# A graph kernel whose attention passes pick three rows in four groups on TensorE, with the weighed values in PSUM and the decays in SBUF

## The reference

```python
h = max(layernorm(x), 0); x = x + sage2(h)             # two passes: sums
h = max(layernorm(x), 0); x = x + transformer2(h)      # two attention passes
h = max(layernorm(x), 0); x = x + graph_transformer(h) # one attention pass, with an edge bias
h = max(layernorm(x), 0); x = x + gin2(h)              # two passes: maxima

# one attention layer
alpha = sum(q[dst] * k[src], -1) * scale     # (edges, 8)
m     = segment_max(alpha, dst)
a     = exp(alpha - m[dst]);  a = a / segment_sum(a, dst)[dst]
out   = segment_sum(v[src] * a[:, :, None], dst)
```

## Time and profile before

| | us |
|---|---|
| median of 3 runs | 8551.9 |
| lowest and highest | 8509.88, 8577.97 |
| the profiled execution | 8522.77 |
| its span | 8520.5 |
| PE busy with matmuls | 5177.5 (29027 matmuls) |
| DVE busy | 5170.0 |
| POOL busy | 4941.0 |
| ACT busy | 2588.6 |

### The profile page before, as it was taken

One profiled execution on the slowest core, in us unless ns is written; L12 is line 12 of the kernel. 1 busy time (PEld: TensorE's weight loads), 2 busy tenths in 40 slices (PEclk: granted clock), 3 DMA queues, 4 the chain that ended last, 5 costly groups with the idle time before them and its releaser, 6 DMA issues.

```text
span 8520.5 us, 85738 instructions
## 1 busy us (share of the span) xinstructions
PE 5177.5 (61%) x29027; PEld 3050.1 (36%) x29027; DVE 5170.0 (61%) x9372; ACT 2588.6 (30%) x6303; POOL 4941.0 (58%) x5102
## 2 busy tenths in 40 slices
PE   4767658887455555355455344454536888768887
PEld 2333334444333333133333233333323444434443
DVE  6666545555677777677777777777773333333333
ACT  3333311111344544354444444444440000000000
POOL 6666665555455665455655555555536555565555
PEclk8777878888777766677766666666657888778887
DMA  4444434444344444344444344444424455445544
GB/s 128 143 140 142 138 118 162 162 163 154 113 145 147 153 148 151 121 146 144 150 145 142 123 142 135 146 134 145 134 72 144 161 162 163 133 142 163 163 162 133
DMA packets 464201, 1216.31 MB, mean 143 GB/s; under 512 B 109489, under 2 KB 142271, under 8 KB 463752
## 3 DMA queue, kind: packets, MB, share of 16 engines
q1 hardware_dynamic: 263180, 721.75, 24.3%
q0 software_dynamic: 200576, 489.04, 20.0%
HBM read 736.73 MB, written 473.62 MB: 142 GB/s over the span
## 4 chain that ended last, share of the span: by engine, by line
PE 43%; issue 31%; DVE 12%; another core or an unknown queue 6%; ACT 4%; DMA 3%; POOL 0%; SPq 0%; DVEq 0%; POOLq 0%; ACTq 0%
PE banks_ps L1630 14%; PE banks_ps L1614 14%; PE cout_ps L1614 5%; PE pair_ps L1614 5%; PE cin_ps L1614 4%; DVE outs L758 2%; ACT outs L1356 1%; DVE hot_both L812 1%; DVE bias L776 1%; DVE work L776 1%; DMA hot_small<-kept_hots 1%; DVE work L896 1%; DMA hot_both<-kept_hots 1%; DVE arena L786 1%
## 5 line engine op out<-in xcount | busy, mean ns | idle before, releaser
L1967 POOL DMA_INDIRECT arena<-table,near_idx x4732 | 4593.8, 971 | 2965.9 <-issue 1412.4
L1614 PE MATMUL banks_ps<-arena,work 128*128 128x384 bf16 x6750 | 1328.1, 348 | 388.1 <-issue 299.4
L1614 PEld LDWEIGHTS banks_ps<-arena,work 128*128 128x128 fp8e4 (+1 forms) x6750 | 681.9, 102 | 988.5 <-issue 624.6
L850 DVE COPY_PREDICATED pair_ps<-near_late,pair_ps 128x896 f32<-128x896 uint8 x336 | 368.5, 1097 | 853.9 <-ACT pair_ps L1375 752.5
L1630 PE MATMUL banks_ps<-arena,hot_small 128*128 128x256 bf16 x2025 | 619.9, 306 | 361.2 <-issue 360.4
L1630 PE MATMUL banks_ps<-work,hot_small 128*128 128x256 bf16 x2025 | 620.5, 306 | 357.8 <-issue 357.0
L896 DVE TENSOR_TENSOR_SCAN work<-banks_ps,work 128x1024 f32<-128x1024 f32 x336 | 769.7, 2291 | 11.5
L786 DVE TENSOR_REDUCE arena<-banks_ps 128x128 f32<-128x384 f32 x324 | 179.6, 554 | 974.1 <-remote 808.2
L1630 PE MATMUL banks_ps<-arena,hot_both 128*128 128x256 bf16 x2025 | 619.8, 306 | 233.4 <-issue 233.0
L1630 PE MATMUL banks_ps<-work,hot_both 128*128 128x256 bf16 x2025 | 618.1, 305 | 229.9 <-issue 229.8
L1299 ACT COPY near_idx<-src_i 128x7 int32<-128x7 int32 x784 | 150.7, 194 | 1953.1 <-DVE outs L758 1713.4
(11 more groups left out here) (267 smaller groups left out, 8634.7 us busy)
## 6 DMA issues: line engine op xcount, KB each, us to landing
rows_plain<-outs SPq DMA_DIRECT2D x448, 448.0 KB
work<-kept_hots SPq DMA_DIRECT2D x432, 400.0 KB
rows_att<-outs SPq DMA_DIRECT2D x336, 504.0 KB
arena<-table,near_idx POOLq DMA_INDIRECT x4732
kept_hots<-hot_small SPq DMA_DIRECT2D x162, 400.0 KB
hot_small<-kept_hots SPq DMA_DIRECT2D x81, 400.0 KB
hot_both<-kept_hots SPq DMA_DIRECT2D x81, 400.0 KB
table<-arena SPq DMA_DIRECT2D x18, 512.0 KB, 3.0
```

What stands on the lines that cost most here:

```text
L850: chain(v.copy_predicated(prod, near_late[:, s, :].unsqueeze(2).to_broadcast(wide), next_q.unsqueeze(1).to_broadcast(wide)))
L1614: ins = pe.matmul(pick_bank[u], hot[:, t, :], parts3[:, :, t, :], start=(t == 0), stop=(t == NB - 1))
L1967: pool.indirect_dma_start(dst, None, tab, bass.IndirectOffsetOnAxis(ap=idx, axis=0))\
```

## The change

`WIDE` goes from [1, 0, 1, 0] to [1, 1, 1, 0], so in iterations 1 to 27 of an attention pass slot 1 gets its last row from PE as well. `msg` was two buffers in SBUF; it is now one, in the two PSUM banks in which `dB` lay. `dB` was one buffer in PSUM; it is now two in SBUF, where `msg` lay. The activation that writes `dB` moves from `decay` in `lay_rows` to the end of `weigh`, and DVE waits for it before the first instruction of `part_b` instead of before the last. The bank of a pick goes by s % 2: the picks of slots 0 and 2 share a bank, those of slot 1 have the other. The passes that are not attention keep their picks (`PICKS`).

```diff
-WIDE = [1, 0, 1, 0]
+WIDE = [1, 1, 1, 0]
 PICKS = {0: [1, 1, 1, 1], 1: [2, 1, 2, 1], 2: WIDE, 3: WIDE, 4: WIDE, 5: [2, 1, 2, 1], 6: [2, 1, 2, 1]}
...
-        msg = [work[:, GD + b * GS:GD + (b + 1) * GS] for b in range(2)]
+        dB = [work[:, GD + b * GS:GD + (b + 1) * GS] for b in range(2)]
...
-        dB = banks_ps[:, 0:GS]
+        msg = banks_ps[:, 0:GS]
...
-                v.wait_ge(s_weigh, g * 3 + (weigh_base[k] + 2))
+                v.wait_ge(s_weigh, g * 3 + (weigh_base[k] + 3))
...
-                chain(v.tensor_tensor(by_edge(msg[b]).rearrange("p j (h c) -> p j h c", c=CH), vals, wts,
+                chain(v.tensor_tensor(by_edge(msg).rearrange("p j (h c) -> p j h c", c=CH), vals, wts,
                                       ALU.mult))
...
-                v.wait_ge(s_weigh, g * 3 + (weigh_base[k] + 3))
-                chain(v.tensor_tensor_scan(OS[b], dB, msg[b], 0.0, ALU.mult, ALU.add))
+                chain(v.tensor_tensor_scan(OS[b], dB[b], msg, 0.0, ALU.mult, ALU.add))
...
                 act.activation(LA[b][:, :, 1:GROUP + 1], DE[:, b, 1, :, :], ACT.Exp).then_inc(s_weigh, 1)
-
-            def decay(b):
-
-                act.activation(dB.rearrange("p (h c t) -> p h c t", h=HEADS, c=CH)[:, :, :, 1:GROUP + 1],
+                act.activation(dB[b].rearrange("p (h c t) -> p h c t", h=HEADS, c=CH)[:, :, :, 1:GROUP + 1],
                                DE[:, b, 0, :, :].unsqueeze(2).to_broadcast([P, HEADS, CH, GROUP]), ACT.Exp)\
                     .then_inc(s_weigh, 1)
...
-                act.copy(column(msg[to], 0), column(OS[1 - to], GROUP)).then_inc(s_on, 1)
+                act.copy(column(msg, 0), column(OS[1 - to], GROUP)).then_inc(s_on, 1)
...
                     carry_on(s, 1 - s % 2)
-                    decay(1 - s % 2)
...
-                    act.copy(ring[:, s, GROUP - 1, :], wide_bank[s // 2]).then_inc(s_whole, 1)
+                    act.copy(ring[:, s, GROUP - 1, :], wide_bank[s % 2]).then_inc(s_whole, 1)
...
-                    if s // 2 in last_in:
-
-                        pe.wait_ge(s_whole, last_in[s // 2])
-                    last_in[s // 2] = pick_number(k, it, s) + 1
+                    if s % 2 in last_in:
+
+                        pe.wait_ge(s_whole, last_in[s % 2])
+                    last_in[s % 2] = pick_number(k, it, s) + 1
```

More of the change, by code:

```diff
@@ L1398, in att_pass @@
                 weigh(k, 0, 0)
-                decay(0)
                 lay_queries(k, 0, 1, 1, far)
@@ L1623, in pick_wide @@
                     pe.wait_ge(s_back8[s], kept_loads(k, it, s))
-                    if s // 2 in last_in:
-                        pe.wait_ge(s_whole, last_in[s // 2])
-                    last_in[s // 2] = pick_number(k, it, s) + 1
+                    if s % 2 in last_in:
+                        pe.wait_ge(s_whole, last_in[s % 2])
+                    last_in[s % 2] = pick_number(k, it, s) + 1
                     for t in range(NB):
                         for a, part in enumerate(split_at[k]):
-                            ins = pe.matmul(wide_bank[s // 2], hot_wide[n % 2][:, t, :], part[:, t, :],
+                            ins = pe.matmul(wide_bank[s % 2], hot_wide[n % 2][:, t, :], part[:, t, :],
                                             start=(t == 0 and a == 0), stop=(t == NB - 1 and a == 2))
```

## The result

The changed kernel took 8980.48 us (median of 4 runs, 8926.04 to 9010.12) against 8557.06 of before beside it: a ratio of 1.0496, 95% interval 1.0461 to 1.0531. The forecast was 9275 with a range of 8600 to 9500. The profiled run has a span of 8996.9 us, 476.4 more than before's.

The account below looks back on a forecast made before the run. PE's picks were taken to set the pace, with PE starved during POOL's long gather runs. The sum: 8522.8 (the profiled run) + 745 (third pick) + 16 (shared bank) - 9 (`msg`) = 9275 us, range 8600 to 9500.

Parts of the forecast that it names:

- PE's picks set the pace: Attention passes: the time from one PE pick to the next bounds an iteration at 45.9 us; DVE and POOL need 35.3.
- The third pick, +745: Attention passes: 81 more picks, 6075 pairs, take an iteration from 43.3 to 52.5 us, +745 us over 81 iterations.
- Starved time by gathers: PE in the attention passes: starved time goes by POOL's gathers, 0.91 us each, so 25.5 us an iteration becomes 24.6.
- the first rival: POOL's runs chopped to six to eight gathers, PE starved in none: +32 to +122 us, near 8600; chance 0.17.
- The shared bank, +16: Slot 0's pick waits for ACT's copy of slot 2's, once an iteration, 0 to 0.4 us each: +16 us.
- `msg` in PSUM, -9: DVE's multiplication into PSUM takes 0.68 us less a group, counting only in some 27 groups: -9 us.
- the decays, 0: ACT's decays into SBUF take 0.9 to 1.8 us, hidden behind DVE's `part_b`: 0 us.
- The faster rival, 7665 us: Attention passes: PE is not starved any more and DVE sets the pace with 35.3 us, -859 us; chance 0.12.

Follow-up runs that it names:

- e8: The change with the third bf16 part left out of the attention passes' picks, so 50 pairs in a pick: 8497.89 us, ratio 0.9991 to before.
- e5: The kernel before, unchanged, profiled on a chip of the experiments where before takes some 8500 us: 8538.99 us, one execution.
- e6: The change, unchanged, on a chip where the kernel before took 8507.6 us: 8843.79 us, ratio 1.041.
- e10: The change, unchanged, once more, on a chip where the kernel before took 8505.0 us: 8807.87 us, ratio 1.0363.
- e7: The kernel before, with POOL made to wait after the gathers of slots 1 and 3 until those rows have landed: 8238.83 us, ratio 0.9694.
- e1: The change with the old `WIDE` [1, 0, 1, 0] and the old banks, so the buffers alone: 6868.36 us, ratio 0.9907 to before.
- e4: The change with `WIDE` [1, 0, 0, 0], one pick in four groups, each one-hot load waiting for the one before: 6969.89 us, ratio 1.0051 to before.
- e11: The change with one pick in four groups and POOL waiting after slot 3's gathers until the rows have landed: 7156.00 us, ratio 1.0326 to before.
- e12: The kernel of e1, the change's buffers alone with two picks in four groups, run once more: 6862.87 us, ratio 0.9903 to before.
- e2: The kernel before with the new `WIDE` and the new banks, so the third pick alone: 6931.83 us, ratio 0.9999.
- e9: The kernel of e3, the change with no picks in the attention passes, where before took 8505.0 us: 8258.22 us, ratio 0.9712.
- e3: The change with `WIDE` [0, 0, 0, 0], no picks in the attention passes, where before took 6933.4 us: 7072.98 us, ratio 1.0202.

## Why the prediction was right, and where its size was off

**PE's picks set the pace: right** on chips like that of the first profile. All of the 478 us are in the attention passes. DVE's 224 us less and POOL's 81 gathers less did not keep them from growing, and e8 shows that the loss follows PE's pairs. The granted clock of the passes went from 0.68 to 0.70 up to 0.73 to 0.74, so it took no part in the loss.

**The third pick, +745: the right mechanism, too large.** The term's "after" was near: it said 52.5 us for an iteration, 24.6 of them starved; the iteration above has 51.2 with 25.6 starved, and the mean is 51.8. What was mis-sized is the "before" that was taken off. The formula gave 43.3, from a piece of 2.5 iterations that was better than the mean of 45.9. I had both numbers in the text and subtracted the wrong one; 52.5 - 45.9 = 6.6, times 81 = 535, would have given 9065. Counted over all 81 iterations, by the gaps between successive weight loads, before has 28.9 us of gaps over 0.3 us in an iteration and 16.9 us with 132 pairs (0.128 each); the change has 25.4 and 26.3 us with 204 (0.129). So the pairs cost 9.4 us more, where I had 10.1. The starved time fell by 3.5 us, where I had 0.9: that is the part of the term that was wrong.

**Starved time by gathers: half right.** It fell more than the gathers did, because POOL's runs were chopped, which was the first rival: in the iteration above 14, 6 and 7 in place of 21 and 7. But that rival had PE starved in none of them, and the run of 14 starves it for 13 us, while 6 and 7 with 1.00 us between act like one run. The piece of the earlier trace rows didn't show the other side of this. It has runs of 21 only, but in 29 stretches of before's passes all 28 gathers of four groups are one run, with gaps too short to help, and there PE's gaps come to a median of 31.8 us. Counted over all 81 iterations of each trace, where gaps and rest are those between PE's weight loads, over 0.3 us and not:

| kernel | POOL's gathers | its pauses over 2.3 us | gaps, us an iteration | rest | sum |
|---|---|---|---|---|---|
| before | 2290 | 97 | 28.9 | 16.9 | 45.9 |
| before again (e5) | 2310 | 99 | 29.4 | 16.8 | 46.2 |
| the change | 2239 | 156 | 25.4 | 26.3 | 51.7 |
| the change (e6) | 2226 | 140 | 24.5 | 25.6 | 50.1 |
| the change (e10) | 2226 | 134 | 24.2 | 25.5 | 49.7 |
| two parts (e8) | 2218 | 103 | 27.5 | 18.4 | 45.9 |
| pauses (e7) | 2290 | 175 | 23.6 | 18.6 | 42.2 |

On the whole, more long pauses go with less starved time, at nearly the same number of gathers. The gaps also hold PE's ordinary waits, which are few where PE sets the pace; in e1, with no starved stretch, they are 14.8 us. The rule that holds for before, the change and e7 is in runs: PE has some 60 to 70 pairs from the start of a run that follows a long pause, then one every 0.7 us or slower, until 2 to 3.5 us after the last gather. e7 shows it as cause. There the stock is also seen to be smaller after a short pause: in the long runs that follow a pause of 2.0 to 2.8 us PE slowed after 22 to 28 pairs (medians), in those after 2.8 us and more, after 63 or more.

**The shared bank, +16: not settled.** PE waited 198.6 us for ACT's copy, 73 times, 2.7 us each, beyond my bound of 0.4. In the iteration above PE's last load of the pick is at 2654.77, ACT's copy runs from 2657.14, and PE goes on at 2657.62, 0.1 us after it. The copy is the last 0.4 us; the 2.4 before it fall into the 2.7 us after POOL's last gather, when PE's signal was late with all else. That is argued from the times. No run gave the third pick a bank of its own, so the price stays open. That e8 takes no longer than before with one pick more speaks for a small one.

**`msg` in PSUM, -9, and the decays, 0: the prices of the two instructions were right.** 1095 ns, as L855 had said; 937 ns, near the lower bound. That the buffers bring nothing where PE starves was not measured by itself; DVE's wait behind ACT grew by 1504 - 753 = 751 us in the change, which is room enough for their 224, and e8 has no gain from them. The Trainium skill (ScalarE: Activation LUTs, Step-by-step: what each stage is for) has ScalarE faster into PSUM than into SBUF; for this operation the difference is 24 ns in 913, so it agrees in sign and cost 8 us of ACT's free time.

**The faster rival, 7665 us:** wrong here, and its mechanism is how the chips of e1 to e4, e11 and e12 work. With PE supplied, the third pick alone gave 0.9999: its gather less can't show while DVE's 35.3 us are the bound. The Trainium skill's rule that instruction fetch is mostly hidden (Runtime: NRT & Kernel Launch, Instruction fetch mechanics) agrees with e2, where 223 loads came in 34 us of gathers. By it PE would not have lacked instructions in the earlier trace rows and e7 either, and there it was held up; whether by fetching them no run shows. My chance for it, 0.12, was a chance about the kernel; it should have been one about the chip, and one trace couldn't tell.

## What to carry to other kernels

Where an engine waits for "issue" in a trace, look at what another engine does at the same time: here it was POOL's run of gathers, and two rests of three microseconds in each iteration gave back 3% of the kernel. Take a difference from the measured mean of the same stretch, not from a formula fitted to a piece of it. And a verdict on a change that trades one engine's instructions for another's may hold on one chip and not on the next: e7, 3% faster on a starving chip, should be slower on another (no run shows it), as e11's one pause in an iteration already cost 186 us there.

## What the runs showed of the hardware

- The same program took 8505 to 8557 us in three measurements (two chips at least) and 6928 and 6933 on two other chips. In e1 and e2, on one of the latter, the attention passes have no starved stretch. The attention passes are only half of the difference: before's took 3715 us, e2's 2903, and outside of them the spans differ by 4805.5 - 4025.4 = 780 us. There too PE waited for "issue" before its weight loads (L1614), 1365 us before and 208 in e2. Whether it is the chip itself or something that went on beside the kernel at the time stays open.
- On a starving chip PE got 9 to 14 weight loads in 11 to 21 us, after some 60 to 70 pairs from the start of a run of gathers. How long POOL must rest is sharply marked. Over the attention passes of before, e5, the change, e6, e10 and e7, I took the pauses of POOL in whose last 5 us before them PE had got one to 8 loads. After 116 pauses of 0.6 to 2.4 us PE was back at full pace (over 12 loads in the first 3 us of the next run) 3 times; after 51 of 2.4 to 2.8 us, 42 times; after 523 longer ones, 518 times.
- ACT slowed as well, to 1.4 us from instruction to instruction, after some 40 us of an uninterrupted run (e9, looked at in one place); DVE didn't at that time.
- The profile's queue for instructions moved 3.77 MB before and 4.55 MB in the change: 0.78 MB for 6075 pairs, 128 bytes a pair. A transfer of 16 KB on it took 0.88 to 2.54 us in the change (median 0.98) and 0.88 to 1.71 us in e2 (median 0.97), so such transfers were hardly slower on a starving chip. None of them falls into the starved stretch from 2618.7 to 2632.1, whose 14 pairs need only 1.8 KB; the starving isn't seen on this queue.
- The best kernels measured: e7 with 0.969 and e9 with 0.971 on starving chips, e1 and e12, the buffers alone, with 0.991 and 0.990 on the others. Of these only the kernel of e9 ran on both kinds, and on the other it was 2% slower than before (e3).
